# An expert layer whose network turns are woven between the choosing of rows, and 48 gathers ahead of the first store

## The chip, the cores and the metric

One core of one Trainium2 chip runs the whole program. The metric is the device time of one execution in microseconds (us). The engines are PE (TensorE), DVE (VectorE), ACT (ScalarE), POOL (GpSimd) and SP (SyncE, which only issues transfers here). Each engine works through its own instructions in order and meets the others through semaphores.

## The reference

`x` has 32 rows of 120000 samples. They are cut into 938 frames of 128, each frame is turned by an orthonormal cosine basis, and a linear recurrence over the frames of the normalised result is added. The part that matters here is the third step, on `h` of 32 x 938 = 30016 rows of 128:

```python
x_flat = x.reshape(N, Dd)                      # x is the layernorm of h
logits = x_flat @ Wr                           # 8 experts
probs = jax.nn.softmax(logits, axis=0)         # over all rows
vals, idx = jax.lax.top_k(probs.T, C)          # 1024 rows for each expert
selected = x_flat[idx]
h = jax.nn.gelu(jnp.einsum('ecd,edf->ecf', selected, W1) + b1[:, None, :], approximate=False)
out_e = jnp.einsum('ecf,efd->ecd', h, W2) + b2[:, None, :]
weighted = vals[..., None] * out_e
output = jnp.zeros_like(x_flat).at[idx.reshape(-1)].add(weighted.reshape(-1, Dd))
```

Every expert picks its own 1024 rows, so a row can be picked by several experts and the last step is a sum.

## The kernel before

Up to about 350 us the kernel turns, normalises and filters the rows, stores `h` to `out`, and finds for each expert the score at which exactly 1024 rows are in: 13 rounds of counting (`count_round`, L1507 to L1530; the last eight are phase 1). A copy `kept` of `out` is made in the meantime, from which rows are gathered later. The change lies almost wholly in what follows.

The expert part knows 8 experts in 4 pairs, and an expert's 1024 rows as 8 tiles of 128 in two halves `q` of 4 tiles.

- **Choosing.** `extract(pair)` on DVE marks the rows in (two compares L1573), numbers them by a scan (L1576), waits for the PE sums of `offsets(pair)` and makes each row's rank (L1583 to L1603), then `mark(e)` builds a one-hot table for each of the two experts (L1562). PE's `differences(pair)` (L1093) and ACT's `own_steps(pair)` (L822) turn the ranks to steps, PE's `ranks(e, q)` (L1107, eight matmuls) multiplies them with the one-hot table, and `choose(e)` on DVE (L1614 to L1624) makes of each half four columns of `index`.
- **Gathering.** POOL's `find(n)` (L1829) is an indirect DMA of 128 rows from `kept` to `found`. It waits for its half of `index`.
- **Network.** `moments_of_found(e)` on DVE (L1632 to L1662, with many tiny steps) needs the eight gathers of the expert, `normalise_rows(e)` on ACT (L829) follows, `ffn_turn(n)` on PE (L1118) turns half an expert, `turned(n)` on ACT (L837) copies it, `up(n)` on PE (L1133) makes four blocks of 128x512, `gelus(n)` on ACT (L848) takes them one by one, and `down(n)` on PE (L1146) is 16 products of 128x128 summed over four. `score_of_found(e)` on DVE (L1670 to L1677) and `weights_of` on ACT (L854, L855: an exponential between two loads of function tables) make the softmax weights, and `answer(e, g)` on DVE (L1683 to L1698) adds the bias and multiplies with the weights.
- **Adding.** POOL's `add(e)` issues eight indirect DMAs to `out`: expert 0 stores (L1846), the others accumulate (L1843), and each waits until all earlier ones have landed, because two experts may hold the same row.

The order is written out by hand on every engine. Before the change DVE does pairs 0, 1 and 2 whole, then `softmax_scales`, the moments of expert 0, pair 3, expert 6, and then the networks; half 0 and half 1 of expert 7 are chosen between the answers of experts 1 to 3. PE does the same: all choosing first (with `ranks(7, .)` left out), then for each expert `up, up, down, ffn_turn, down`. ACT has the exponential over all scores (`far`, L861) after `own_steps` of pairs 0 to 2. POOL issues 54 gathers, then `add(0)`, then two gathers after each `add`.

## Time and profile before

| | us |
|---|---|
| time, median of 3 executions | 600.93 |
| lowest and highest | 600.62, 605.86 |
| the profiled execution, first to last instruction (span) | 605.3 |
| of it up to the first gather on POOL | 362.5 |
| from there to the end of the last accumulating DMA's issue | 235.0 |
| from there to the end of the span | 7.8 |
| busy share of the span: PE, DVE, ACT, POOL | 66%, 70%, 48%, 49% |

The profile is one execution. Busy times are of the engine, a gap before an instruction is shown in brackets with what ended it, and "remote" or "another core or an unknown queue" means that the semaphore rose at a moment at which no recorded instruction ended. A time of an instruction is from the start of the span.

### The profile page before, as it was taken

How to read it: one execution, taken by the hardware profiler on the slowest of the kernel's cores; microseconds unless marked ns; L12 is line 12 of the kernel's file. 1: busy time of each engine (PE TensorE's matmuls, PEld its weight loads, DVE VectorE, ACT ScalarE, POOL GpSimd, SP SyncE). 2: the span in 40 equal slices, each digit the busy share in tenths (PEclk: the TensorE clock that was granted, in tenths of full speed). 3: DMA queues.
4: the chain of work that ended last, by engine and by line, in shares of the span. 5: the costliest groups of instructions: out<-in, count | busy, mean ns of one | idle time of the engine just before them, and what ended most of it. 6: DMA issues, size and time to landing. Idle time of an engine off the chain costs nothing.

```text
span 605.3 us, 11347 instructions
## 1 busy us (share of the span) xinstructions
PE 397.3 (66%) x3577; PEld 320.0 (53%) x3577; DVE 425.8 (70%) x1653; ACT 292.2 (48%) x560; POOL 298.7 (49%) x213
## 2 busy tenths in 40 slices
PE   5798898999888889997000033210199989997900
PEld 5786788865877788764000022110057667775700
DVE  3877878898488887898888878911787658866100
ACT  2787840076699740177545500120258667686400
POOL 0467830058478730076000007776235687888774
PEclk9999999999899999999555555555579989999965
DMA  8679606699888227699999501121011344443332
GB/s 162 132 183 272 150 15 162 142 253 241 194 148 148 58 48 157 201 275 254 323 318 318 190 0 44 49 52 48 17 28 61 67 74 67 65 75 44 31 30 22
DMA packets 86116, 77.44 MB, mean 128 GB/s; under 512 B 15022, under 2 KB 82930, under 8 KB 85810
## 3 DMA queue, kind: packets, MB, share of 16 engines
q1 hardware_dynamic: 68674, 64.52, 41.6%
q0 software_dynamic: 10368, 8.40, 9.8%
q10 hardware_dynamic: 7024, 3.89, 2.7%
q8 instruction: 27, 0.44, 0.3%
q14 instruction: 23, 0.19, 0.1%
HBM read 52.27 MB, written 39.39 MB: 151 GB/s over the span
## 4 chain that ended last, share of the span: by engine, by line
PE 32%; DVE 21%; issue 14%; DMA 10%; POOL 10%; ACT 6%; another core or an unknown queue 5%; SPq 1%; ACTq 1%; DVEq 0%; POOLq 0%
PE banks L1003 7%; POOL out L1843 7%; PE banks L1030 5%; PE banks L929 5%; PE banks L1133 4%; PE banks L1146 4%; PE banks L1040 3%; DMA xin<-in_x 3%; ACT xn L680 2%; PE banks L915 2%; DMA ring<-toeplitz 2%; DVE xn L1512 2%; DMA const<-constants 1%; DVE xn L1576 1%
## 5 line engine op out<-in xcount | busy, mean ns | idle before, releaser
L1829 POOL DMA_INDIRECT hid<-kept,index x64 | 65.0, 1015 | 115.6 <-DVE index L1624 97.0
L1214 DVE BATCH_NORM_STATS2 stats<-hid 120x6 f32<-120x128 f32 (+1 forms) x512 | 104.9, 278 | 19.8 <-ACT hid L671 19.4
L1843 POOL DMA_INDIRECT out<-hid,index x56 | 88.6, 1582 | 25.9 <-issue 16.3
L929 PE MATMUL banks<-const,xt 128*120 128x128 f32 x512 | 74.0, 290 | 12.0 <-ACT xt L666 11.5
L775 ACT ACTIVATE xt<-banks 128x480 f32<-128x480 f32 x64 | 36.3, 570 | 84.9 <-PE banks L1030 83.7
L929 PEld LDWEIGHTS banks<-const,xt 128*120 128x120 f32 x512 | 63.9, 192 | 20.7 <-ACT xt L666 14.4
L1751 POOL TENSOR_TENSOR small<-small,powers 120x16 f32<-120x16 f32 (+2 forms) x18 | 47.9, 2662 | 47.1 <-DVE small L1232 47.1
L1819 POOL TENSOR_TENSOR small<-small,powers 120x16 f32<-120x16 f32 x15 | 43.2, 2901 | 41.7 <-DVE small L1232 36.3
L1003 PE MATMUL banks<-xn,ring 122*120 122x128 f32 x512 | 58.9, 276 | 6.3 <-DMA xn<-s 3.1
L1146 PEld LDWEIGHTS banks<-w_ring,xn 128*128 128x128 f32 x512 | 60.5, 196 | 3.9 <-issue 3.9
L1003 PEld LDWEIGHTS banks<-xn,ring 122*120 122x120 f32 x512 | 57.6, 189 | 7.4 <-issue 6.9
L1146 PE MATMUL banks<-w_ring,xn 128*128 128x128 f32 x512 | 61.2, 279 | 0.4 <-issue 0.4
L1133 PE MATMUL banks<-xt,w_ring 128*128 128x512 f32 x128 | 61.2, 613 | 0.0
L848 ACT ACTIVATE xn<-banks,b_cols 128x512 f32<-128x512 f32 x64 | 43.6, 687 | 28.4 <-PE banks L1133 25.0
L1415 DVE TENSOR_TENSOR hid<-hid,banks 120x512 f32 (+1 forms) x64 | 42.5, 685 | 11.4 <-PE banks L1003 10.7
L829 ACT ACTIVATE xn<-hid,xn 128x128 f32<-128x128 f32 x64 | 25.5, 481 | 43.1 <-issue 36.0
L671 ACT ACTIVATE hid<-banks 120x512 f32<-120x512 f32 (+1 forms) x64 | 37.9, 592 | 12.1 <-PE banks L929 12.0
L666 ACT ACTIVATE xt<-banks 128x480 f32<-128x480 f32 x64 | 37.4, 588 | 10.0 <-PE banks L915 10.0
L1070 PE MATMUL banks<-counts,setup 128*128 128x3 f16 x13 | 2.4, 187 | 60.4 <-DVE counts L1522 60.4
L915 PE MATMUL banks<-const,xin 120*128 120x120 f32 x256 | 37.8, 277 | 5.6 <-DMA xin<-in_x 5.3
L680 ACT ACTIVATE xn<-hid,small 120x128 f32<-120x128 f32 (+1 forms) x80 | 39.7, 597 | 1.9 <-DVE small L1333 1.8
L1030 PE MATMUL banks<-const,hid 120*128 120x120 f32 x256 | 39.2, 277 | 1.9 <-DVE hid L1415 1.0
(222 smaller groups left out, 705.1 us busy)
## 6 DMA issues: line engine op xcount, KB each, us to landing
kept<-out SPq DMA_DIRECT2D x1, 15008.0 KB, 50.5
xin<-in_x SPq DMA_DIRECT2D x28, 480.0 KB, 6.9
out<-hid SPq DMA_DIRECT2D x14, 960.0 KB, 11.1
w_ring<-in_L_ffn_W SPq DMA_DIRECT2D x16, 256.0 KB
ring<-toeplitz SPq DMA_DIRECT2D x32, 112.5 KB
toeplitz<-ring SPq DMA_DIRECT2D x6, 545.0 KB, 11.3
out<-hid SPq DMA_DIRECT2D x2, 784.0 KB
xin<-in_x SPq DMA_DIRECT2D x4, 384.0 KB
```

The lines of the kernel that those rows point to most:

```text
L680: ins = act.activation(xn[0:L, :, bass.ds(c * HB + b, 1)].rearrange("p k a -> p (k a)"), hid[:, bass.ds(c * HB + b, 1), :].rearrange("p a ...
L848: act.activation(acts[:, g, f], banks[:, 1 + f, :], ACT.Gelu, bias=b1_cols[:, FC * e + f:FC * e + f + 1]).then_inc(gelu_ready, 1)
L915: mm = pe.transpose(spread_rows[:, a, f], xin[:, n // 4, 2 * (n % 4) + a, f * D:(f + 1) * D], cut["identity"][0:L, 0:L].rearrange("p (q j) ...
L929: mm = pe.matmul(banks[0:L, 2 + n % 4, i * D:(i + 1) * D], xt[:, n % 2, i, :], cut["basis_t"], start=True, stop=True)
L1003: mm = pe.matmul(banks[0:L, 2 + n % 4, q * COLS:(q + 1) * COLS], lags[:, slot, (4 * (n % 2) + q) // WOVEN, 0:L, (4 * (n % 2) + q) % WOVEN] ...
L1030: mm = pe.transpose(banks[:, n % 2, j * L:(j + 1) * L], hid[:, c * HB + 4 * j + n, :], cut["identity"][0:L, 0:L])
L1133: pe.matmul(banks[:, 1 + f, :], w1_ring[:, e % 2, f * P:(f + 1) * P], xt_all[:, g], start=True, stop=True).then_inc(up_ready, 1)
L1146: mm = pe.matmul(banks[:, 5 + g, m * D:(m + 1) * D], acts[:, g, f, m * P:(m + 1) * P], w2_ring[:, e % 2, f, :], start=f == 0, stop=f == FC ...
L1214: ins = dve.bn_stats(stats[:, slot, b, :], hid[:, bass.ds(c * HB + b, 1), :].rearrange("p a k -> p (a k)"))
L1751: pool.tensor_tensor(small[:, slot, 4, columns], small[:, slot, 2, columns], powers[0:L, columns], ALU.pow).then_inc(done, 1)
L1829: pool.indirect_dma_start(found[:, n, :], None, kept, bass.IndirectOffsetOnAxis(ap=index[:, n:n + 1], axis=0)).then_inc(found_in[e], 16)
L1843: pool.indirect_dma_start(rows, at_rows, adds[:, n, :], None, compute_op=ALU.add, oob_is_err=True, bounds_check=ROWS * FRAMES - 1).then_in ...
```

## The change

- **The order on DVE.** `extract` is split in `number(pair)` (compares and scan) and `rank_rows(pair)` (the rest). Pairs 0 and 1 are chosen first, then the moments of expert 0, experts 2 and 3, and from there choosing and networks alternate: pair 2 is numbered between the two answers of expert 0, pair 3 after the score of expert 2. From expert 3 on it is answer, answer, score of the next, moments of the one after.
- **The order on PE and ACT.** PE's calls are written out one by one in the same alternation: `offsets(2)` stands behind `up(2)`, `differences(2)` behind `up(3)`, `offsets(3)` behind `up(4)`, `differences(3)` behind `up(5)`. On ACT `own_steps(2)` and `own_steps(3)` stand behind the gelus of experts 1 and 2, `weights_of` is called once for each expert right behind its gelus (before: in five single calls and two double ones with some of them later), and `normalise_rows` of the next expert stands behind it.
- **The order on POOL.** 48 gathers, `add(0)`, the 8 gathers of expert 6, `add(1)`, the 8 gathers of expert 7, then the other adds with nothing between them.
- **The minimum over all scores.** The reduction of 1920 elements on DVE (L1481) is made in eight pieces of 240, one in each round of phase 1; the minimum of the eight pieces follows where the long one stood, which is now behind the first pair's `rank_rows`.
- **Buffers.** The cutoffs are copied from PSUM to SBUF once (`cut_offs`); `normed` has a place of its own; the steps and offsets of pairs 2 and 3 and the ranks of experts 4 to 7 go through bank 7, so `differences(2)` and `(3)` wait until all earlier ranks are used; `up(0)` waits at its fourth block for the copy of the scales (`spread_taken`).

```diff
 BOUND_MARGIN, BOUND_FLOOR = 1.01**2, 1e-12
 NEAREST_OF_BOUND = 0.98 * (1 - 1 / 1.01)
-FOUND_FIRST = 54
-WEIGHED_AFTER = {3: (3, 5), 5: (5, 7), 6: (7, 8)}
-FOUND_BETWEEN = 2
+FOUND_FIRST = 48
+NEAR_PIECES = 8
+NEAR = SEG // NEAR_PIECES
+RANK_COLS = 4 * (L + 2)
 COPIED_ROWS = 512
 RING, SLOTS = 8, 4
 TURN = RING * SLOTS
...
@@ -285,8 +286,7 @@
         acts = xn_all[:, :, :].rearrange("p a b -> p (a b)")[:, 0:2 * FC * 512].rearrange(
             "p (s f n) -> p s f n", s=2, f=FC)
         gone = take("xn", TB * L).rearrange("p (a b) -> p a b", b=L)
-        normed_at = free["xn"][1]
-        work = [take("xn", TB * L) for _ in range(4)]
+        work = [take("xn", TB * L) for _ in range(3)]

         upper, lower = (work[0].bitcast(U16)[:, n * SEG:(n + 1) * SEG] for n in range(2))
         marks = [seen.bitcast(U16)[:, n * SEG:(n + 1) * SEG] for n in range(2)]
@@ -309,6 +309,8 @@
...
+        near = sb("near", [P, NEAR_PIECES])
+        cut_offs = sb("cut_offs", [P, E])
...
@@ -327,13 +328,19 @@
         fstats = take("xn", SLOT_TILES * 6).rearrange("p (m n) -> p m n", m=SLOT_TILES)
         fsmall = take("xn", 3 * 7 * SLOT_TILES).rearrange("p (s n m) -> p s n m", s=3, n=7)
         banks = ctx.enter_context(nc.psum_tensor("banks", [P, 8, 512], F32))
-        def offsets_bank(pair):
-
-            return 0 if pair < PAIRS - 1 else 5
+        def offsets_of(pair):
+
+            if pair < 2:
+                return banks[:, 0, 16 * pair:16 * pair + 10]
+            return banks[:, 7, RANK_COLS + 10 * (pair - 2):RANK_COLS + 10 * (pair - 1)]
+
+        def steps_bank(pair):
+
+            return 1 + pair if pair < 2 else 7

         def rank_bank(e, q):

-            return 6 if q and e < E - 1 else 7
+            return 6 if q and e < 4 else 7

         def logit_bank(c):

...
@@ -854,31 +862,24 @@
                 act.activation(parts[:, first:end, :], scores[:, first:end, :], ACT.Exp).then_inc(weight_ready, end - first)
                 act.activation(sc[:, 7:8], sc[:, 7:8], ACT.Gelu)

-            for pair in range(PAIRS - 1):
-                own_steps(pair)
+            own_steps(0)
             act.wait_ge(far_out, 32)
             act.wait_ge(nearest_ready, 1)
             act.activation(far, far, ACT.Exp, scale=-1.0, bias=sc[:, 10:11], accum_out=sc[:, 4:5]
                            ).then_inc(sum_ready, 1)
             act.activation(sc[:, 7:8], sc[:, 7:8], ACT.Gelu)
+            own_steps(1)
             normalise_rows(0)
             turned(0)
-            own_steps(PAIRS - 1)
             for e in range(E):
                 gelus(2 * e)
-                if e == 1:
-                    weights_of(1, 2)
                 gelus(2 * e + 1)
-                if e == 2:
-                    weights_of(2, 3)
+                if e in (1, 2):
+                    own_steps(e + 1)
+                weights_of(e, e + 1)
                 if e < E - 1:
                     normalise_rows(e + 1)
-                if e == 0:
-                    weights_of(0, 1)
-                if e < E - 1:
                     turned(2 * e + 2)
-                if e in WEIGHED_AFTER:
-                    weights_of(*WEIGHED_AFTER[e])

         @block.tensor
         def _(pe):
@@ -1075,7 +1076,7 @@
             def offsets(pair):

                 pe.wait_ge(totals_ready, pair + 1)
-                into = banks[:, offsets_bank(pair), 16 * pair:16 * pair + 10]
+                into = offsets_of(pair)
                 last = numbered[:, pair, :, :, L - 1:L].rearrange("p k (e h) a -> p h k (e a)", h=2)
                 pe.matmul(into[:, 0:8], half["before"],
                           numbered[:, pair, :, :, L - 1:L].rearrange("p k c a -> p (k c a)"), start=True, stop=False)
...
@@ -1088,8 +1089,10 @@
                 pe.wait_ge(rank_ready, pair + 1)
                 if pair == 0:
                     pe.wait_ge(base_ready, 2)
+                if pair > 1:
+                    pe.wait_ge(row_used, 4 * pair)
                 ranked = rank[:, 4 * pair:4 * pair + 4, :]
-                into = banks[:, 1 + pair, 0:4 * (L + 2)]
+                into = banks[:, steps_bank(pair), 0:RANK_COLS]
                 pe.matmul(into, half["steps"], ranked.rearrange("p a b -> p (a b)"), start=True, stop=False)
                 pe.matmul(into.rearrange("p (e h t) -> p h e t", h=2, t=L + 2)[:, 1], half["wrap"],
                           ranked.rearrange("p (e h) t -> p h e t", h=2)[:, 0], start=False, stop=True
@@ -1100,8 +1103,8 @@
                 if q == 0:
                     pe.wait_ge(onehot_ready, e + 1)
...
-                if e:
-                    pe.wait_ge(row_used, 2 * e + q - (0 if q and e == E - 1 else 1))
+                if e or q:
+                    pe.wait_ge(row_used, 2 * e + q - (1 if e < 4 else 0))
...
                     if n:
                         pe.wait_ge(gelu_ready, FC * (n - 1) + f + 1)
+                    elif f == FC - 1:
+                        pe.wait_ge(spread_taken, 1)
...
                 if n == 1:
-                    pe.wait_ge(row_used, 2 * E - 2)
+                    pe.wait_ge(row_used, 8)
...
-            for pair in range(PAIRS):
-                if pair == 2:
-                    pe.wait_ge(peak_ready, 1)
-                    pe.matmul(banks[:, 4, 0:P], cut["group"], peaks, start=True, stop=True).then_inc(peak_spread, 1)
-                if pair == 3:
-                    pe.wait_ge(sum_ready, 1)
-                    pe.matmul(banks[:, 4, P:P + 1], cut["group"], sc[:, 4:5], start=True, stop=True).then_inc(sum_spread, 1)
-                    pe.wait_ge(spread_in_ready, 2)
-                    pe.matmul(banks[:, 4, 2 * P:2 * P + 2 * E], cut["ones"],
-                              spread_in[:, 1:3, :].rearrange("p a b -> p (a b)"),
-                              start=True, stop=True).then_inc(spread_done, 1)
-                    ffn_turn(0)
-                offsets(pair)
-                differences(pair)
-                for e in (2 * pair, 2 * pair + 1):
-                    if e < E - 1:
-                        for q in range(2):
-                            ranks(e, q)
-            for e in range(E):
...
+            offsets(0)
+            differences(0)
+            ranks(0, 0)
+            peaks_of_group()
+            ranks(0, 1)
+            ranks(1, 0)
+            ranks(1, 1)
+            offsets(1)
+            sum_of_group()
+            differences(1)
+            ranks(2, 0)
+            scales_of_experts()
+            ranks(2, 1)
+            ffn_turn(0)
+            ranks(3, 0)
+            up(0)
+            ranks(3, 1)
+            up(1)
+            down(0)
+            down(1)
+            ffn_turn(2)
+            up(2)
+            offsets(2)
+            up(3)
+            differences(2)
+            ranks(4, 0)
+            down(2)
+            ranks(4, 1)
+            down(3)
+            ranks(5, 0)
+            ranks(5, 1)
+            ffn_turn(4)
+            up(4)
+            offsets(3)
+            up(5)
+            differences(3)
+            ranks(6, 0)
+            down(4)
+            down(5)
+            ranks(6, 1)
+            ffn_turn(6)
+            up(6)
+            ranks(7, 0)
+            up(7)
+            ranks(7, 1)
+            down(6)
+            down(7)
+            for e in range(4, E):
+                ffn_turn(2 * e)
                 up(2 * e)
-                if e == 0:
-                    ranks(E - 1, 0)
                 up(2 * e + 1)
-                if e == 3:
-                    ranks(E - 1, 1)
                 down(2 * e)
-                if e < E - 1:
-                    ffn_turn(2 * e + 2)
                 down(2 * e + 1)

         @block.vector
@@ -1478,7 +1524,7 @@

             def nearest_of_partitions():

-                dve.tensor_reduce(sc[:, 0:1], far, AX.X, ALU.min).then_inc(dve_own, own.one())
+                dve.tensor_reduce(sc[:, 0:1], near[:, :], AX.X, ALU.min).then_inc(dve_own, own.one())
                 dve.wait_ge(dve_own, own.all())
                 dve.tensor_scalar(peaks, cut["identity"], sc[:, 0:1], -1.0, ALU.mult, ALU.mult).then_inc(peak_ready, 1)

@@ -1521,6 +1567,9 @@
                     dve.tensor_scalar(counts[:, 0:1], sc[:, 13:14], 1.0 / PACK, None, ALU.mult)
                     dve.tensor_tensor(counts[:, 1:2], sc[:, 12:13], sc[:, 13:14], ALU.subtract
                                       ).then_inc(count_ready, 1)
+                    if phase:
+                        dve.tensor_reduce(near[:, columns(i, 2, k, 1)], far[:, columns(i, 2 * NEAR, k * NEAR, NEAR)],
+                                          AX.X, ALU.min).then_inc(dve_own, own.one())
                     dve.wait_ge(count_spread, turn - phase)

                     dve.scalar_tensor_tensor(passed[:, :], banks[:, 4, 0:3], wanted_below,
@@ -1532,7 +1581,7 @@
...
-            def extract(pair):
+            def number(pair):

                 cols = slice(4 * pair, 4 * pair + 4)
                 both = lambda a: a.rearrange("p (e h) l -> p e (h l)", h=2)
                 flat = lambda a: a.rearrange("p k c l -> p (k c l)")
-                cutoff = banks[:, 5, 2 * pair:2 * pair + 2].unsqueeze(2).broadcast_to([P, 2, 2 * L])
+                cutoff = cut_offs[:, 2 * pair:2 * pair + 2].unsqueeze(2).broadcast_to([P, 2, 2 * L])
...
+
+            def rank_rows(pair):
+
+                cols = slice(4 * pair, 4 * pair + 4)
                 dve.wait_ge(offsets_ready, pair + 1)
                 by_expert = lambda a: a.rearrange("p (e h) -> p e h", h=2)
                 below_in_front, equal_in_front, below_in_all = (
-                    banks[:, offsets_bank(pair), 16 * pair + a:16 * pair + b] for a, b in ((0, 4), (4, 8), (8, 10)))
+                    offsets_of(pair)[:, a:b] for a, b in ((0, 4), (4, 8), (8, 10)))
                 left = wanted[:, pair, :].unsqueeze(2).broadcast_to([P, 2, 2])
                 dve.tensor_scalar(wanted[:, pair, :], below_in_all, -1.0, float(CAP), ALU.mult, ALU.add
                                   ).then_inc(dve_own, own.one())
@@ -1595,10 +1648,6 @@
...
-                if pair == 3:
-                    pe.wait_ge(sum_ready, 1)
-                    pe.matmul(banks[:, 4, P:P + 1], cut["group"], sc[:, 4:5], start=True, stop=True).then_inc(sum_spread, 1)
-                    pe.wait_ge(spread_in_ready, 2)
...
-            for pair in range(PAIRS - 1):
-                if pair == 2:
-                    nearest_of_partitions()
-                extract(pair)
-                if pair == 2:
-                    nearest_of_experts()
-                choose(2 * pair)
-                choose(2 * pair + 1)
+            def take_scales():
+
+                dve.wait_ge(spread_done, 2)
+                dve.tensor_copy(spread[:, :, :].rearrange("p a b -> p (a b)"),
+                                banks[:, 4, 2 * P:2 * P + 2 * E]).then_inc(spread_taken, 1)
+                dve.wait_ge(spread_taken, 1)
+
+            dve.tensor_copy(cut_offs[:, :], banks[:, 5, 0:E]).then_inc(dve_own, own.one())
+            dve.wait_ge(dve_own, own.all())
+            number(0)
+            rank_rows(0)
+            nearest_of_partitions()
+            choose(0)
+            nearest_of_experts()
+            choose(1)
+            number(1)
+            rank_rows(1)
             softmax_scales()
             moments_of_found(0)
-            extract(PAIRS - 1)
-            choose(E - 2)
+            choose(2)
+            take_scales()
+            choose(3)
+            score_of_found(0)
             moments_of_found(1)
-            score_of_found(0)
-            for e in range(E):
-                if e == 1:
-                    score_of_found(1)
-                    moments_of_found(2)
-                if e == 2:
-                    score_of_found(2)
-                    choose(E - 1, (0,))
-                    moments_of_found(3)
-                if e == 3:
-                    score_of_found(3)
-                    moments_of_found(4)
-                    score_of_found(4)
+            answer(0, 0)
+            number(2)
+            answer(0, 1)
+            rank_rows(2)
+            choose(4)
+            choose(5)
+            score_of_found(1)
+            answer(1, 0)
+            answer(1, 1)
+            moments_of_found(2)
+            score_of_found(2)
+            number(3)
+            rank_rows(3)
+            moments_of_found(3)
+            choose(6, (0,))
+            answer(2, 0)
+            choose(6, (1,))
+            answer(2, 1)
+            choose(7)
+            score_of_found(3)
+            moments_of_found(4)
+            for e in range(3, E):
                 answer(e, 0)
                 answer(e, 1)
-                if e == 3:
-                    choose(E - 1, (1,))
-                if e >= 3 and e + 2 < E:
+                if e + 1 < E:
+                    score_of_found(e + 1)
+                if e + 2 < E:
                     moments_of_found(e + 2)
-                    score_of_found(e + 2)

         @block.gpsimd
         def _(pool):
@@ -1850,13 +1918,11 @@
             pool.wait_ge(kept_in, 16)
             for n in range(FOUND_FIRST):
                 find(n)
-            n = FOUND_FIRST
             for e in range(E):
                 add(e)
-                for _ in range(FOUND_BETWEEN):
-                    if n < E * SLOT_TILES:
-                        find(n)
-                        n += 1
+                first = FOUND_FIRST + e * SLOT_TILES
+                for n in range(first, min(first + SLOT_TILES, E * SLOT_TILES)):
+                    find(n)
             pool.wait_ge(added, 128 * E)
```

## Rows read from the trace of the kernel before

**Rows 1.** The page, part 4: the chain that ended last, shares of the span by engine.

```profile
PE 32%; DVE 21%; issue 14%; DMA 10%; POOL 10%; ACT 6%; another core or an unknown queue 5%; SPq 1%; ACTq 1%; DVEq 0%; POOLq 0%
```

**Rows 2.** POOL's instructions grouped by line: count | busy, mean ns | idle before.

```profile
L1843 POOL DMA_INDIRECT out<-hid,index x56 | 88.6, 1582 | 25.9 <-issue 16.3 <-DMA out<-hid,index 4.9 <-DVE hid L1694 4.7
L1829 POOL DMA_INDIRECT hid<-kept,index x64 | 65.0, 1015 | 115.6 <-DVE index L1624 97.0 <-issue 18.6
```

**Rows 3.** POOL in order of time: start, us, instruction [idle before <- releaser].

```profile
362.53 1.24 POOL L1829 DMA_INDIRECT hid<-kept,index  x1 [79.15 <-DVE index L1624]
...
367.84 2.84 POOL L1829 DMA_INDIRECT hid<-kept,index  x1 [0.30 <-issue]
...
427.98 0.94 POOL L1829 DMA_INDIRECT hid<-kept,index  x1 [6.92 <-DVE index L1624]
...
443.55 0.94 POOL L1829 DMA_INDIRECT hid<-kept,index  x1 [10.89 <-DVE index L1624]
...
459.38 1.02 POOL L1846 DMA_INDIRECT out<-hid,index  x1 [8.65 <-DVE hid L1698]
...
476.17 1.61 POOL L1843 DMA_INDIRECT out<-hid,index  x1 [3.78 <-DVE hid L1694]
...
565.84 1.55 POOL L1843 DMA_INDIRECT out<-hid,index  x1 [2.44 <-DMA out<-hid,index]
...
595.93 1.56 POOL L1843 DMA_INDIRECT out<-hid,index  x1 [0.30 <-issue]
```

**Rows 4.** DVE in order of time: a counting gap, a pair extracted, a half chosen, the minimum.

```profile
349.40 0.22 DVE L1526 SCALAR_TENSOR_TENSOR passed<-banks,sc,const 128x3 f32<-128x3 f32 x1 [0.39 <-PE banks L1070]
...
351.41 1.22 DVE L1573 TENSOR_TENSOR xn<-xn,banks 128x480 f16<-128x480 f32 x2 [0.89 <-PE banks L1073]
352.66 2.16 DVE L1576 TENSOR_TENSOR_SCAN xn<-xin,xn 128x960 f16<-128x960 f16 x1
...
357.17 1.67 DVE L1562 TENSOR_SCALAR ring<-setup,bounds 128x1024 f16<-128x1024 f16 x4
359.87 0.66 DVE L1614 TENSOR_TENSOR xin<-banks,const 128x480 f32<-128x480 f32 x1 [1.03 <-PE banks L1107]
...
361.54 0.65 DVE L1614 TENSOR_TENSOR xin<-banks,const 128x480 f32<-128x480 f32 x1
...
381.67 2.15 DVE L1481 TENSOR_REDUCE sc<-far 128x1 f32<-128x1920 f32 x1
```

**Rows 5.** DVE in order of time: pair 2's halves, the moments of expert 0.

```profile
399.34 0.66 DVE L1614 TENSOR_TENSOR xin<-banks,const 128x480 f32<-128x480 f32 x1 [5.05 <-remote]
...
425.95 0.66 DVE L1614 TENSOR_TENSOR xin<-banks,const 128x480 f32<-128x480 f32 x1 [11.54 <-remote]
...
428.09 1.64 DVE L1632 BATCH_NORM_STATS2 xn<-hid 128x6 f32<-128x128 f32 x8
...
432.96 0.17 DVE L1662 SCALAR_TENSOR_TENSOR xn<-xn 128x8 f32<-128x8 f32 x1
```

**Rows 6.** PE in order of time: the ranks of pair 2, then half networks.

```profile
391.51 2.86 PE L1107 MATMUL banks<-xin,ring 128*128 128x122 f16 x24 [0.71 <-DVE ring L1562]
...
455.57 3.74 PE L1146 MATMUL banks<-w_ring,xn 128*128 128x128 f32 x32
459.21 2.81 PE L1133 MATMUL banks<-xt,w_ring 128*128 128x512 f32 x6
```

**Rows 7.** ACT and DVE groups by line, window 440 to 578 us: count | busy, mean ns | idle before.

```profile
L829 ACT ACTIVATE xn<-hid,xn 128x128 f32<-128x128 f32 x56 | 22.3, 481 | 7.1 <-DVE xn L1662 7.0
L854 ACT ACT_TABLE_LOAD x6 | 7.7, 1283 | 0.1
L1670 DVE SCALAR_TENSOR_TENSOR hid<-hid,xn,wr_all 128x128 f32<-128x128 f32 x64 | 24.5, 445 | 0.0
```

**Rows 8.** Windows: stretch, us, busy of PE, PEld, DVE, ACT, POOL (count), PEclk, DMA, GB/s.

```profile
392.00:426.00 34.00, 3.60 (x31) 3.03 (x29) 5.18 (x19) 4.76 (x5) 22.05 (x24) 0.50 0.18 46
446.00:470.00 24.00, 24.00 (x141) 16.97 (x140) 18.38 (x96) 20.46 (x36) 12.07 (x12) 1.00 0.19 56
```

22 lines of the change are left out of this document (15 added, 7 removed).

## The prediction

> **What bounds the kernel now.** I read the chain that ended last first [rows 1]: PE, DVE and POOL share it, and 5% of it, some 28 us, belongs to no instruction. The chain taken for the last 120 us is POOL's queue alone, so the second view is POOL in order of time [rows 3]. From the first gather (362.53) to the end of the last issue (595.93 + 1.56 = 597.49) are 235.0 us. Its work, with the 0.30 between two issues: 64 gathers at 0.94 + 0.30 = 1.25 are 80.0; 8 stores at 1.02 + 0.30 are 10.6; 56 accumulating ones at 1.55 + 0.30 = 1.86 are 104.2. That is 194.8. Its waits beyond the 0.30: for `index` 6.6 and 10.6, for answers 8.4 and 3.5, together 29.1; for earlier adds to land twice 2.1, so 4.3. The rest, 6.8, are stretched issues, such as the gather of 2.84 at 367.84. So the end of the kernel is POOL's work plus what POOL starves for, and only the starving can be changed.
>
> **Where the starving comes from.** All of it goes back to DVE in pair 2 [rows 5]: three halves begin after waits of 5.05, 11.5 and 11.54 us (the middle one has no row), in sum 28, with "remote" as releaser. PE's matmuls for these halves stand in the trace at 391.51 (24 of them in 2.86 us) [rows 6]; their semaphore rose only when DVE went on. I call this the hold. PE had 3.6 us of work in these 34, at a granted clock of 0.50, the lower level [rows 8]. The gathers went on beside it, so POOL lost less than 28 there, but the moments of expert 0 began at 428.09 [rows 5] instead of near 400, and with them `add(0)`.
> The Trainium skill ("SBUF — State Buffer", Who interferes with whom) says that PE and ACT never wait on anyone for SBUF; this trace shows PE's results late by 28 us, and which resource held them it does not show.
>
> **The change, part by part.**
> *Start.* The copy of the cutoffs adds 0.2 on the path to the first gather. The eight partial minima: 1920 elements took 2.15 at L1481, so 240 take about 0.3, in a gap of 0.39 in which DVE waits for PE's count [rows 4]; hidden at best, 8 x 0.1 = 0.8 if the gap ends late. The long one of 2.15 is gone, the short minimum with its scaling (0.5) stands in the 1.03 before the first half of choosing [rows 4]. I take +0.4: first gather at 362.9.
> *POOL.* The same 64, 8 and 56 issues: 194.8. Gathers of experts 6 and 7 now cover the landing of adds 0 and 1; adds 3 to 7 follow on adds without cover, 5 x 2.2 = 11.0 against 4.3. Stretched issues: 6.8 as before. A bare landing wait is the 2.44 of [rows 3] less 0.30. Busy means of the two kinds of issue: [rows 2]. Bare end: 362.9 + 194.8 + 11.0 + 6.8 = 575.5, and 7.8 to the end of the span: 583.3. To this comes what POOL starves for.
> The long gather of 2.84 began beside pair 1's scan on DVE, and pair 3's scan ran while POOL was idle; now every scan runs beside POOL: one more stretch, 0 to 2, inside the 6.8.
> The Trainium skill (same page and section) lets a DVE instruction with two SBUF inputs contend with GpSimd reads; the long gather agrees. By that rule the sum would be 2 us longer at most.
> *Units of the chain.* A pair: compares and scan 3.4, `rank_rows` 2.1 to the ranks and 1.6 for the one-hot tables [rows 4]. PE `differences` 0.8, ACT `own_steps` 0.6, PE `ranks` 0.4 at the upper level and 0.8 at the lower. Half a choosing: 1.67 from start to start [rows 4], its index after 1.75. Moments 5.0 [rows 5]. Score 8 x 0.38 and two small ones, 3.4; `normalise_rows` 3.2, `weights_of` 2 x 1.28 and two short ones, 3.0 [rows 7]. `down` 3.6, `up` with the turn 4 x 0.9 + 0.4 = 4.0, twice that for both at the lower level of the clock [rows 6, 8]. Answer 1.4, for expert 0 1.8.
> *Up to index 4.* Pair 0 ends at 359, experts 0 and 1 are chosen by 367.6, pair 1 is ready at 375. The moments of expert 0 wait for its eighth gather (8 x 1.25 and the stretched one after 362.9, plus 2.4 to land, as in [rows 3]: 377) and end at 382. Expert 2 is chosen by 385.3. The second half of expert 3 now stands behind `up(0)` on PE: rows normalised from 382, turned from 383.8, PE at the lower level, so about 391, chosen by 393. Then score 0 and moments 1: 401.5. Answer 0, the numbering of pair 2 and answer 0's second half: 409. PE in the meantime: turn 2 at 403.7, `up(2)` to 410; only behind it `offsets(2)`, the ranks at 412.5, `up(3)` with its gelus to 415.3, `differences(2)`, `own_steps(2)`, `ranks(4, 0)`, half a choosing: index 4 at about 418.5. POOL has issued 32 gathers by 362.9 + 40.0 + 3.2 = 406.1. **It starves 12 us.** The other three halves of experts 4 and 5 come every 2 to 4 us, POOL needs one every 5: no wait. Stalled behind the late index are all later gathers and `add(0)`, whose answers are long there.
> *Up to index 6.* 16 gathers and `add(0)` take POOL from 418.5 to 449. DVE: experts 4 and 5 chosen by 428.5, score 1 to 432, answer 1 waits for `weights_of(1)` (3.0), moments 2 to 441, score 2, numbering of pair 3 to 448. ACT stood in `weights_of(1)` until score 1 was there, so the rows of expert 2 are normalised only from 441; turn, `up(4)` on a PE that idled since 428 and starts at the lower level: 450.5; `offsets(3)`, ranks 453, `up(5)` 454; on DVE moments 3 stand in front of `choose(6)`: 459; index 6 at 460. **It starves 11 us.** Index 7 (469) is before the end of `add(1)` (485), and the answers are 20 us and more ahead of their adds from here.
> *Sum.* 583.3 + 12 + 11 = 606 in the span of a profiled execution, against 605.3. The layout saves 28 + 1 (the old starving) and pays 23 of new starving, 6.7 of bare landings and 0.4: a draw. If both clocks are at the upper level throughout, 2 x 3 less: 600. The median of 600.93 is 4.3 under the profiled span; I give the new kernel half of that: 604.
>
> **The rivals.**
> *Faster: the indices come in time.* If index 4 is there by 406 and index 6 by 449 minus the 12 gained, the span is 583.3, 3.6% less; with one of them, 594 to 595. For it: DVE and PE are busy under two thirds in the stretch and PE may run each network faster than my 16 us. Against: `offsets(2)` stands behind `up(2)`, which stands behind moments 1, and these behind score 0; the chain is 12 us too long. It decides where index 4 comes before 410: under 598.
> *Slower: the hold falls on the new chain.* It is a property of this program's traffic, not of the order, or the usual executions of before had less of it than the profiled one. Then up to 28 us are added one to one if it falls between 375 and 460, since every PE step there leads to index 4 or 6; after 470 the answers have 20 us of slack and it costs nothing. 604 + 8 to 28: 612 to 632. For it: gathers run beside PE the whole time, as in the hold. Against: pairs 0 and 1 met no hold beside the same gathers.
> *Slower: PE's clock stays at the lower level.* PE now has short bursts with idle time between them from 383 to 470; before it was continuous from 440 and had 1.00 from 446 [rows 8]. At the lower level throughout up to 470 the chain to index 4 has `up(0)`, `down(0)`, `down(1)`, `up(2)` and `up(3)` longer by 18 us and the one to index 6 by 10: 630; half of it: 617.
> *No change by the partial minima alone.* They are 2.15 us in front of pair 2, now off the path; they can't be told apart.
>
> **How the numbers follow.** The draw (598 to 611) 0.45, of which 0.03 lies under 594.9 and 0.08 over 606.9; the faster rival 0.20; the hold 0.22; the low clock 0.13. A measurement of this kernel can tell about 1%, so faster is under 594.9, slower over 606.9. Faster 0.23, same 0.34, slower 0.43. Predicted is the draw's 604. The range takes in half of the fast rival and most of the slow ones: 588 to 626, which leaves out 0.2. The draw's own range is 598 to 611.
>
> **What would show it.** POOL's waits: one before gather 33 and one before gather 49 with `index` as releaser, of 8 to 15 us each, and five of about 2.2 before adds 3 to 7. No wait of POOL for an answer. DVE's wait before the second half of expert 3 of 4 to 7 us with PE L1107 as releaser. "Remote" waits under 5 us in all; if they are over 10 between 375 and 460, the hold rival holds. A granted clock of 0.50 between 410 and 470 speaks for the clock rival. I am wrong if POOL waits for neither index (then 583 to 595), or if the first gather is later than 364.

## The result, and the profile after

| | before | after |
|---|---|---|
| time, median, us | 601.4 | 623.7 |
| lowest and highest | 600.6, 605.9 | 622.3, 624.2 |
| the profiled execution's span | 605.3 | 622.2 |
| first gather on POOL | 362.5 | 361.4 |
| from there to the end of the last add's issue | 235.0 | 252.1 |
| from there to the end of the span | 7.8 | 8.7 |

The ratio is 1.036, with a 95% interval of 1.032 to 1.040. The change makes the kernel slower by 22 us, against the 604 that I named as likeliest. That is outside the draw's own 598 to 611 and inside the 612 to 632 of the rival in which the hold falls on the new chain. (The 600.93 of the first table was the median of three of these four executions of the kernel before.)

All of it is on POOL after the first gather. Its three groups by line (after; count | busy, mean ns | idle before), the answer to [rows 2]:

```profile
L1911 POOL DMA_INDIRECT out<-hid,index x56 | 88.4, 1579 | 28.1 <-issue 15.5 <-DMA out<-hid,index 12.5
L1897 POOL DMA_INDIRECT hid<-kept,index x64 | 63.6, 993 | 139.9 <-DVE index L1673 121.0 <-issue 18.9
L1914 POOL DMA_INDIRECT out<-hid,index x8 | 9.2, 1152 | 2.4 <-issue 2.4
```

The busy time is that of before: 161.2 against 161.9 us. The waits for an index are 121.0 less the 79.5 in front of the first gather, 41.5; before they were 97.0 less 79.15, 17.9. The waits for an answer, 13.3 before, are gone. The waits for landings are 12.5 against 4.9. So +23.6, -13.3 and +7.6, and less than 1 by busy and issue time: 17.1 us, which is 252.1 - 235.0. POOL of after in order of time, the answer to [rows 3]:

```profile
361.37 1.24 POOL L1897 DMA_INDIRECT hid<-kept,index  x1 [79.50 <-DVE index L1673]
...
403.97 0.95 POOL L1897 DMA_INDIRECT hid<-kept,index  x1 [5.78 <-DVE index L1673]
...
429.22 0.95 POOL L1897 DMA_INDIRECT hid<-kept,index  x1 [20.34 <-DVE index L1673]
...
442.76 0.95 POOL L1897 DMA_INDIRECT hid<-kept,index  x1 [3.85 <-DVE index L1673]
...
476.02 1.00 POOL L1897 DMA_INDIRECT hid<-kept,index  x1 [11.56 <-DVE index L1673]
...
529.74 1.55 POOL L1911 DMA_INDIRECT out<-hid,index  x1 [2.40 <-DMA out<-hid,index]
...
598.91 1.55 POOL L1911 DMA_INDIRECT out<-hid,index  x1 [2.50 <-DMA out<-hid,index]
```

Two waits stand where I had put them, before gathers 33 (429.22) and 49 (476.02), and five landings are bare (the first and the last are shown). Two waits are new: before gather 29 (the second half of expert 3) and before gather 41 (expert 5). What is late in front of them stands on DVE, the answer to [rows 5]:

```profile
386.41 0.66 DVE L1663 TENSOR_TENSOR xin<-banks,const 128x480 f32<-128x480 f32 x1 [3.27 <-remote]
...
401.95 0.66 DVE L1663 TENSOR_TENSOR xin<-banks,const 128x480 f32<-128x480 f32 x1 [13.78 <-remote]
...
440.73 0.66 DVE L1663 TENSOR_TENSOR xin<-banks,const 128x480 f32<-128x480 f32 x1 [7.72 <-remote]
```

That is 24.8 us of "remote" waits up to 460; before had 28. A fourth of 7.86 ends at 519.35, where no add waits for it. And ACT, which takes the blocks of `up(0)`, sees the same:

```profile
389.87 0.69 ACT L856 ACTIVATE xn<-banks,b_cols 128x512 f32<-128x512 f32 x1 [6.46 <-PE banks L1138]
394.10 0.69 ACT L856 ACTIVATE xn<-banks,b_cols 128x512 f32<-128x512 f32 x1 [3.54 <-remote]
398.30 0.69 ACT L856 ACTIVATE xn<-banks,b_cols 128x512 f32<-128x512 f32 x1 [3.51 <-remote]
401.81 0.60 ACT L845 ACTIVATE xt<-banks 128x512 f32<-128x512 f32 x1 [2.83 <-remote]
402.31 0.68 ACT L856 ACTIVATE xn<-banks,b_cols 128x512 f32<-128x512 f32 x1
```

The blocks reach ACT 4.2 us apart; I had counted 1.8 for one at the lower clock. The windows of this stretch and of the next (after; columns as in [rows 8]):

```profile
383.50:402.00 18.50, 6.79 (x20) 3.20 (x20) 1.66 (x6) 2.25 (x4) 11.34 (x12) 0.68 0.17 46
402.00:430.00 28.00, 25.82 (x137) 17.37 (x138) 21.31 (x82) 18.14 (x30) 4.77 (x5) 0.88 0.10 29
```

In the first 18.5 us every engine but POOL stands nearly still beside 12 gathers, and with the last of those gathers PE is busy again. That is the hold of [rows 5, 8] in another place.

### The profile page after: what moved, and what is told of

Same layout as the page of the kernel before. It is cut to its first block, busy times and chain, and to the rows that moved or that the text cites. A ratio compares the mean times of both kernels' runs of the same rounds, so it can differ in the third digit from the quotient of the medians.

```text
span 622.2 us, 11373 instructions
## 1 busy us (share of the span) xinstructions
PE 398.7 (64%) x3577; PEld 318.2 (51%) x3577; DVE 426.5 (69%) x1662; ACT 298.5 (48%) x568; POOL 298.1 (48%) x213
## 4 chain that ended last, share of the span: by engine, by line
PE 28%; issue 21%; DVE 14%; POOL 13%; DMA 12%; ACT 7%; SPq 2%; another core or an unknown queue 2%; ACTq 1%; DVEq 0%; POOLq 0%
POOL out L1911 10%; PE banks L1004 6%; PE banks L1031 5%; PE banks L930 4%; PE banks L1138 4%; PE banks L1041 3%; DMA out<-hid,index 3%; DMA xin<-in_x 3%; DMA ring<-toeplitz 2%; ACT xn L688 2%; PE banks L916 2%; DVE xn L1558 2%; POOL hid L1897 2%; DMA const<-constants 1%
## 5 line engine op out<-in xcount | busy, mean ns | idle before, releaser
L1897 POOL DMA_INDIRECT hid<-kept,index x64 | 63.6, 993 | 139.9 <-DVE index L1673 121.0
L1138 PE MATMUL banks<-xt,w_ring 128*128 128x512 f32 x128 | 68.9, 678 | 18.4 <-ACT xt L845 12.1
L1151 PEld LDWEIGHTS banks<-w_ring,xn 128*128 128x128 f32 x512 | 58.3, 192 | 2.7 <-issue 2.7
L1151 PE MATMUL banks<-w_ring,xn 128*128 128x128 f32 x512 | 58.8, 275 | 0.0
L1138 PEld LDWEIGHTS banks<-xt,w_ring 128*128 128x128 f32 x128 | 25.6, 216 | 47.9 <-issue 33.3
```

The source lines that it names most:

```text
L1138: pe.matmul(banks[:, 1 + f, :], w1_ring[:, e % 2, f * P:(f + 1) * P], xt_all[:, g], start=True, stop=True).then_inc(up_ready, 1)
L1151: mm = pe.matmul(banks[:, 5 + g, m * D:(m + 1) * D], acts[:, g, f, m * P:(m + 1) * P], w2_ring[:, e % 2, f, :], start=f == 0, stop=f == FC ...
L1897: pool.indirect_dma_start(found[:, n, :], None, kept, bass.IndirectOffsetOnAxis(ap=index[:, n:n + 1], axis=0)).then_inc(found_in[e], 16)
```

## The experiments

The runs were made on four chips, here A to D, and the kernel before ran beside them on each. One reading has to stand in front. **The kernel before takes 578.6 us on chip A and 578.0 on D, but 605.9 on B and 605.2 on C** (7, 11, 13 and 1 executions; 576 to 582 on the first two, 602 to 609 on B). The first pair of measurements (601.4 and 623.7) is like B and C. A comparison is therefore only made within one chip. Each chip was used in one sitting only, so the runs do not tell the chip itself from what else went on there at that time; "chip" stands for both.

### Chip A: four variants

**e1: the gathers only after the choosing of experts 0 to 5.**

```diff
             pool.wait_ge(kept_in, 16)
+            pool.wait_ge(index_ready, 12)
```

> The kernel before, but POOL waits until the rows of pairs 0 to 2 are all chosen (index_ready 12) before its first gather, so no gather runs while PE makes the ranks of pair 2. Theory G, the hold on PE needs gathers in flight: DVE's three waits of 28 us in pair 2 shrink to under 1, the twelfth index is there at about 398, 54 gathers follow until about 468, and since POOL's remaining work after them was 142 us, the span is about 611 and the time 613. Theory P, the hold belongs to this place of the program and not to the gathers: the waits stay near 28, the gathers start at about 428 and the time is about 642.

Measured: 610.0 us, one execution, the first gather at 395.15, no "remote" wait of PE's readers. That agrees with theory G, that the hold needs gathers beside PE. But none of the other three runs on this chip has such a wait either, so the run decides nothing by itself; e9 repeats it.

**e2: 28 of the gathers as plain transfers** of consecutive rows, so that the experts' rows are other ones for gathers 17 to 44.

```diff
             def find(n):
...
+                if 16 <= n < 44:
+                    pool.dma_start(found[:, n, :], kept[n * P:(n + 1) * P, :]).then_inc(found_in[e], 16)
+                    return
```

> The kernel before, but the gathers 16 to 43 are plain transfers of 128 consecutive rows of the copy, also issued by POOL (so experts 2 to 5 work on other rows than they should; the work is the same). Theory G1, any transfer from POOL's queue into SBUF at this rate holds PE: the 28 us stay, time near 601. Theory G2, it is the indirect form (an index read and 128 single descriptors): the remote waits in pair 2 fall under 5 us, pair 3 and the answers come 20 us or more earlier and the time falls to about 575 to 585.

Measured: 576.6 us, one execution, 2 under the kernel before on this chip, no hold. Sixteen plain transfers took 9.07 us, where sixteen gathers take 20. POOL gave the time back in waits of 9.04 for an index, 8.85 and 3.00 for answers. It says nothing on the hold, since this chip shows none, but something on the kernel before: without a hold its first answer is there at 430.01 and not at 459.38 [rows 3], and its 54 gathers (67.5 us from about 361.5) fill just the time up to there. This is inferred: no trace of the unchanged kernel was taken on chip A.

**e3: POOL's new order in the kernel before.**

```diff
-FOUND_FIRST = 54
+FOUND_FIRST = 48
...
-            n = FOUND_FIRST
...
-                for _ in range(FOUND_BETWEEN):
-                    if n < E * SLOT_TILES:
-                        find(n)
-                        n += 1
+                first = FOUND_FIRST + e * SLOT_TILES
+                for n in range(first, min(first + SLOT_TILES, E * SLOT_TILES)):
+                    find(n)
```

> The kernel before with POOL's new order alone: 48 gathers, add 0, the gathers of expert 6, add 1, those of expert 7, then add 2 to 7. By my prediction's ledger: the six gathers no longer in front of add 0 would let it start earlier, but its answers come at 459.4 only, so POOL just waits there; six gathers of 1.25 move behind it (+7.5), and five bare landing waits of 2.2 replace two and some shorter ones (+6): 614 in all, with experts 6 and 7 gathered earlier than before and so no wait for their answers. If the landing cover and the place of the gathers were worth nothing: 601.

Measured: 601.2 us against 578.6, a ratio of 1.038 (1.032 to 1.043). The loss of 22.6 is more than the 13 I expected, and its terms are on POOL:

```profile
430.56 1.02 POOL L1846 DMA_INDIRECT out<-hid,index  x1 [3.32 <-DVE hid L1698]
...
485.19 0.94 POOL L1829 DMA_INDIRECT hid<-kept,index  x1 [13.79 <-DVE index L1624]
...
508.06 1.55 POOL L1843 DMA_INDIRECT out<-hid,index  x1 [2.54 <-DMA out<-hid,index]
...
576.45 1.55 POOL L1843 DMA_INDIRECT out<-hid,index  x1 [2.49 <-DMA out<-hid,index]
```

Five bare landings instead of two are 7.6, the wait before the stores 3.3, and 13.8 come because all gathers of expert 7 now stand behind `add(1)`, while DVE of the kernel before chooses the second half of expert 7 only between later answers. That is 24.7, 2 more than the loss. The order on POOL is thus no part that could be taken over by itself: the landings cost 7.6, and the rest is lost where the indices are late.

**e4: the changed kernel with a pause.** POOL waits before gather 17 until experts 0 to 3 are chosen.

```diff
             def find(n):
...
                 if m % 4 == 0:
                     pool.wait_ge(index_ready, 2 * e + m // 4 + 1)
+                if n == 2 * SLOT_TILES:
+                    pool.wait_ge(index_ready, 8)
```

> The changed kernel, but POOL makes no gather of experts 2 and up before the rows of expert 3 are all chosen (index_ready 8), which leaves PE's first network without gathers beside it. Theory G: the remote waits before the two halves of expert 3 (3.3 and 13.8 us) go, its last index comes at about 391 instead of 403.7, POOL resumes there and has issued 32 gathers at about 412, index 4 comes 11 us earlier than 429, unless the hold strikes up(1) and down(0) instead; time 612 to 616. Theory O, the order alone made the kernel slower: the pause of 8 us in POOL comes on top or is absorbed by the later wait, and the time stays at 624 or above.

Measured: 609.1 us, one execution, without a hold. Since e2 and e3 have none on this chip either, the pause gets no credit for that. The run is worth more for another thing: it shows the changed kernel's chain undisturbed. POOL:

```profile
364.18 1.23 POOL L1899 DMA_INDIRECT hid<-kept,index  x1 [79.52 <-DVE index L1673]
...
394.58 1.19 POOL L1899 DMA_INDIRECT hid<-kept,index  x1 [8.59 <-DVE index L1673]
...
419.32 0.94 POOL L1899 DMA_INDIRECT hid<-kept,index  x1 [3.03 <-DVE index L1673]
...
461.77 0.99 POOL L1899 DMA_INDIRECT hid<-kept,index  x1 [10.19 <-DVE index L1673]
```

Counted from the first gather, index 4 lets gather 33 go after 55.1 us and index 6 gather 49 after 97.6. The prediction had 418.5 - 362.9 = 55.6 and 460 - 362.9 = 97.1. In after they are 67.9 and 114.7: the hold adds 12.7 and 17. The 12.7 stand in DVE's rows: the two halves of expert 3 wait 3.27 + 13.78 in after and 0.34 + 4.04 in e4.

### Chip B: the changed kernel again, and its order on POOL

**e5: the changed kernel, unchanged.**

> The changed kernel once more, on the chip on which its relatives are timed, since the kernel before took 578.6 us on one chip and 601.4 on another. Theory H (the hold, PE's results 25 to 28 us late beside the gathers, is there in some executions and not in others, and costs both kernels about as much): without a hold the time is that of the paused variant (609.1) less its later start of 2.8, so 606, range 600 to 609; with a hold 624. Against a kernel before without a hold (578.6) that is a ratio of 1.04 to 1.05, and with a hold on both sides 1.036. Rival B (the change is slower only because the hold falls on its new chain): without a hold it is at most 1% over the kernel before, 575 to 585.

Measured: 621.0 us against 605.9, a ratio of 1.027 (1.021 to 1.032). The kernel before has its hold here too (e8), DVE of e5 waits 2.41, 14.40 and 7.64 for unknown releasers, POOL 19.36 before gather 33 and 11.44 before gather 49. All this is as in the first measurement, so the hold is no accident of one execution. Two more "remote" waits, of 7.25 and 1.21, end at 485.94 and 488.90, beside and just behind the gathers of expert 6.

**e6: the changed kernel with POOL's old order.**

```diff
-FOUND_FIRST = 48
+FOUND_FIRST = 54
...
-                first = FOUND_FIRST + e * SLOT_TILES
-                for n in range(first, min(first + SLOT_TILES, E * SLOT_TILES)):
-                    find(n)
+            n = FOUND_FIRST
...
+                for _ in range(2):
+                    if n < E * SLOT_TILES:
+                        find(n)
+                        n += 1
```

> The changed kernel with POOL's old order: 54 gathers, the stores, then two gathers after each add; all else is the changed kernel. Theory N (the networks between the choosing make the index of expert 6 late, about 98 us after the first gather, and 48 is there to answer that): POOL waits about 23 us before gather 49 with the first stores still behind it, and only then two landings are bare: 361.4 + 98 + 7.5 + 140 + 4 + 8 = 618 us of span at most, 609 at least; time 611 to 620 without a hold, 627 with one: slower than the changed kernel by 5 or more. Rival P (POOL's new order alone is the loss, as it lost 22 us when put into the kernel before): undoing it gives back 20, so 586 without a hold and 603 with one.

Measured: 627.6 us (623.4 to 630.5), a ratio of 1.035 (1.029 to 1.041) to the kernel before and 6.6 over e5. Theory N holds with its number. POOL waits 24.41 us before gather 49, with the first stores still to come. So in the changed kernel 48 gathers ahead are better than 54, and giving POOL its old order back saves nothing. That the new order of the networks must cost time does not follow: e7 keeps it and changes POOL alone.

This trace shows one thing more. The hold came back behind gather 49, with two halves of expert 7:

```profile
492.90 0.66 DVE L1663 TENSOR_TENSOR xin<-banks,const 128x480 f32<-128x480 f32 x1 [8.65 <-remote]
...
504.97 0.66 DVE L1663 TENSOR_TENSOR xin<-banks,const 128x480 f32<-128x480 f32 x1 [10.31 <-remote]
```

and the windows of it:

```profile
488.00:494.00 6.00, 5.00 (x24) 2.24 (x23) 1.00 (x3) 1.37 (x3) 4.47 (x6) 1.00 0.16 55
494.00:500.00 6.00, 3.26 (x27) 2.68 (x25) 0.62 (x3) 1.38 (x3) 4.78 (x5) 1.00 0.15 44
```

The granted clock is 1.00 there, the upper level, and falls to 0.54 only in 500 to 506, when the hold is on. In e5 it is 1.00 as well over the two late waits (480 to 489). The lower clock of [rows 8] is not what makes the hold.

**e7: other places for the adds.** 32 gathers, `add(0)`, 16 gathers, `add(1)`, then 4 gathers after each of adds 1 to 4.

```diff
-FOUND_FIRST = 48
+FOUND_FIRST = 32
+FOUND_AFTER = {0: 16, 1: 4, 2: 4, 3: 4, 4: 4}
...
-                first = FOUND_FIRST + e * SLOT_TILES
-                for n in range(first, min(first + SLOT_TILES, E * SLOT_TILES)):
+            n = FOUND_FIRST
...
+                for _ in range(FOUND_AFTER.get(e, 0)):
                     find(n)
+                    n += 1
```

> The changed kernel with another order on POOL only: 32 gathers, add 0, 16 gathers, add 1, then 4 gathers after each of adds 1 to 4. Theory N (POOL starves before gathers 33 and 49, and the adds are bare behind): add 0 (10.6) fills the first wait, add 1 (14.9) the second, and three of the five bare landings of 2.2 are covered. Without a hold the waits left are 4 before add 0 and 5 before gather 49: span 583, time 585, range 580 to 592; with a hold 602. Rival Q (the answers of experts 0 and 1 are later than I read them, or the stores are slowed by the networks beside them): POOL waits before add 0 and add 1 instead, over 10 us each, and the time is within 1% of the changed kernel.

Measured: 602.0 us (599.4 to 606.1, 10 executions), ratio 0.9945 (0.991 to 0.998) to the kernel before, so half a percent, and 19 us under the changed one. POOL:

```profile
414.56 1.14 POOL L1915 DMA_INDIRECT out<-hid,index  x1 [5.86 <-DVE hid L1748]
...
427.33 0.99 POOL L1898 DMA_INDIRECT hid<-kept,index  x1 [1.49 <-DVE index L1674]
...
473.98 1.02 POOL L1898 DMA_INDIRECT hid<-kept,index  x1 [6.58 <-DVE index L1674]
```

The wait of 19.4 before gather 33 has become 5.9 before the stores and 1.5 before the gather, with the stores done in between; the one before gather 49 fell from 11.4 to 6.6, and three landings are covered. The indices are hardly earlier by it (427.33 is 65.9 after the first gather, 66.6 in e5). The changed order had its early answers to give, and 48 gathers in front of the first store let them lie.

**e8: the kernel before, for its trace.**

> The kernel before, unchanged, to have its trace on this chip. If there is no hold here: no wait with an unknown releaser over 2 us between 380 and 480, POOL's waits for an index or an answer under 3 us in all, span 575 to 578. If there is a hold: some 28 us of such waits on DVE and a span of 600 to 605.

Measured: 606.4 us, span 604.6, with the hold in the same places and sizes as in [rows 5]:

```profile
398.79 0.66 DVE L1614 TENSOR_TENSOR xin<-banks,const 128x480 f32<-128x480 f32 x1 [5.10 <-remote]
413.46 0.66 DVE L1614 TENSOR_TENSOR xin<-banks,const 128x480 f32<-128x480 f32 x1 [12.92 <-remote]
425.37 0.66 DVE L1614 TENSOR_TENSOR xin<-banks,const 128x480 f32<-128x480 f32 x1 [10.16 <-remote]
```

### Chip C: what the hold needs

**e9: e1 once more.**

> The kernel before with POOL waiting, ahead of its first gather, for the twelfth half of the index (experts 0 to 5 chosen), once more, on another chip. It took 610.0 on a chip where the kernel before took 578.6. If the kernel before shows the hold on this chip (over 600): theory G (the hold is something that happens to PE beside the gathers) expects no wait with an unknown releaser in the choosing, the first gather at 395 to 398 and 608 to 614 us, for once as much as on the other chip; theory T (it comes at that time of the program, gathers or not) expects 28 us of such waits before the first gather, which comes at 420 or later, and 635 or more. If the kernel before shows no hold here, this repeats 610.

Measured: 636.9 us against 605.2, one execution each. Neither theory comes out whole. On the mechanism G is right: from the first half of pair 0 to the last half of expert 5 the choosing takes 37.51 us here (360.07 to 397.58) and 37.52 in e1 on chip A, with no unknown wait. The first gather is at 400.22 and not at 395.15 because this execution is 5.1 us later already at the first half. But the time is what T said. The hold starts after the gathers have, and goes on through the 54 of them, now beside pair 3 and the moments of expert 0:

```profile
433.94 0.66 DVE L1614 TENSOR_TENSOR xin<-banks,const 128x480 f32<-128x480 f32 x1 [9.53 <-remote]
454.93 0.66 DVE L1614 TENSOR_TENSOR xin<-banks,const 128x480 f32<-128x480 f32 x1 [19.19 <-remote]
...
461.22 0.17 DVE L1646 SCALAR_TENSOR_TENSOR xn<-xn 128x8 f32<-128x8 f32 x1 [2.23 <-remote]
...
464.03 0.17 DVE L1651 TENSOR_SCALAR xn<-xn 128x8 int32<-128x8 int32 x1 [1.93 <-remote]
...
466.82 0.18 DVE L1656 TENSOR_TENSOR xn<-xn 128x8 f32<-128x8 f32 x1 [2.54 <-remote]
...
469.62 0.17 DVE L1660 SCALAR_TENSOR_TENSOR xn<-xn 128x8 f32<-128x8 f32 x1 [1.93 <-remote]
```

The stores then wait 21.1 us for the first answer. The last four lines wait for DVE's own semaphore, with no work of PE in it. So it is not PE's arithmetic that is held. The same steps are 0.20 us apart at 413.92 to 416.77, beside gathers too, before the hold.

**e10: idle PE filled.** Matmuls that nothing uses, ahead of the offsets and ranks of pairs 1 and 2 of the kernel before.

```diff
+            def fill(count):
+
+                for _ in range(count):
+                    pe.matmul(banks[:, 0, 128:512], half["ones"], keep[:, :, :].rearrange("p a b -> p (a b)")[:, 0:384],
+                              start=True, stop=True)
...
+                if pair in (1, 2):
+                    fill(12)
                 offsets(pair)
...
                         for q in range(2):
+                            if pair in (1, 2):
+                                fill(4)
                             ranks(e, q)
```

> The kernel before with work for PE that nothing uses: 12 matmuls of 384 columns ahead of the offsets of pairs 1 and 2, and 4 ahead of each ranks call of these pairs (0.6 us for four at the upper clock, 1.3 at the lower). Nothing is left out. On a chip with the hold: theory I (the hold comes because PE idles beside the gathers, at the lower clock) expects a granted clock of 1.00 in pair 2, unknown waits under 5 us and 582 to 588 us; theory M (each matmul beside the gathers takes some 1.6 us more, whatever the clock; the trace with the old POOL order shows waits of 8.7 and 10.3 at a clock of 1.00) expects the same 25 to 30 us of such waits or more and 603 to 625. On a chip without it: 579 to 585 by both.

Measured: 595.8 us against 605.2, one execution each. Inconclusive. There are still four "remote" waits on DVE up to 434, of 3.37, 9.43, 4.05 and 4.31, 21 in sum, and the granted clock in pair 2 lay between 0.59 and 0.79 in windows of 8 to 14 us, not at 1.00. More matmuls did not make the hold longer, as theory M wanted. Theory I asked for a clock of 1.00 there, and that was not reached, so it is not tested by this run; what speaks against it are the waits of e6 at 1.00.

**e11: the changed kernel a third time.**

> The changed kernel, for the case that this chip is one on which the kernel before takes 578. Theory H (the hold costs both kernels about as much) then expects 600 to 609, a ratio of 1.04 to 1.05, POOL waits for the index of 8 to 12 us before gather 33 and about 10 before gather 49, and five landing waits of 2.5; rival B (the change is slower only through the hold) 575 to 585. With a hold here: 620 to 625.

Measured: 625.0 us against 605.2. This chip has the hold, so the question for which the run was meant, the changed kernel without one, was not answered. The waits are those of after: 18.63 before gather 33, 12.48 before gather 49.

### Chip D: one step of the order undone

**e12: pair 2 chosen right behind pair 1**, on top of e7, with 46 gathers, `add(0)`, 2 gathers, `add(1)`, then four after each of adds 1 to 4. On DVE:

```diff
             choose(3)
-            score_of_found(0)
-            moments_of_found(1)
-            answer(0, 0)
             number(2)
-            answer(0, 1)
             rank_rows(2)
             choose(4)
             choose(5)
+            score_of_found(0)
+            moments_of_found(1)
+            answer(0, 0)
+            answer(0, 1)
             score_of_found(1)
```

On PE `offsets(2)` stands behind `ranks(3, 1)` and `differences(2)` with expert 4 behind `up(1)`; ACT's `own_steps(2)` follows.

> The changed kernel with two things moved. Pair 2 is chosen right behind pair 1 on every engine (numbering, ranks and both experts ahead of the score of expert 0 and the moments of expert 1; on PE its offsets stand behind the second half of expert 3 and not behind the third half network), and POOL issues 46 gathers, add 0, 2 gathers, add 1, then 4 gathers after each of adds 1 to 4. Theory S (the late index of expert 4 comes from where pair 2's offsets stand in the order) expects: without a hold index 4 at 402 to 405, no wait of POOL before gather 33, under 5 before gather 49, 576 to 584 us, within 1% of the kernel before; with a hold 12 to 15 us of wait at gather 33 instead of 19 to 20, some 3 at gather 49, the answers of expert 0 later by 10 to 20, 590 to 598, faster than the kernel before by 1 to 2.5%. Rival D (the order does not matter, since DVE has the same work up to index 4 and 6): the woven variant's time again, 0.99 to 1.00 of the kernel before with a hold.

Measured: 592.7 us (591.7 to 595.0, 6 executions) against 578.0 on this chip, which has no hold: a ratio of 1.026 (1.022 to 1.029), where I expected 576 to 584. POOL:

```profile
359.51 1.23 POOL L1898 DMA_INDIRECT hid<-kept,index  x1 [79.53 <-DVE index L1674]
...
437.25 1.61 POOL L1912 DMA_INDIRECT out<-hid,index  x1 [2.92 <-DVE hid L1744]
...
465.22 1.03 POOL L1898 DMA_INDIRECT hid<-kept,index  x1 [12.20 <-DVE index L1674]
```

The first half of theory S holds: no wait before gather 33, nor for the first stores. The second fails: index 6 comes 105.7 us after the first gather, 8 later than in e4, and POOL waits 12.2 for it instead of less than 5. What pair 2 gained, pair 3 lost, since its numbering stands behind the same scores, moments and answers. With both pairs in front, as the kernel before has them, POOL met no wait in its first 48 gathers on chip A (e3).

## Why the prediction was right or wrong

**Number and mechanism.** 623.7 lies in the stated 588 to 626 only because the range took in most of the slow rivals. The draw, which had the largest chance and gave the 604, did not come; it is 20 us off. The rival of the hold, given 0.22, came, and with it the forecast is right in its second choice and not in its first.

**The first gather**: 362.9 predicted, 361.4 measured (359.3 to 364.2 in the runs of the changed order). The partial minima cost nothing that shows.

**POOL's ledger** held. Bare landings 5 x 2.2 are 12.5 less 5 x 0.3, 11.0; stretched issues 5.9 against 6.8 (pair 1's scan beside a gather of 2.38, pair 3's beside a store of 1.82; pair 2's found POOL idle); tail 8.7 against 7.8. Without starving the sum was 583.3, and it would have been 361.4 + 194.8 + 11.0 + 5.9 + 8.7 = 581.8.

**The two starvings** were in their places, but larger, and two more came before gathers 29 and 41: 23 predicted, 40.3 measured (41.5 less four times 0.3), 17 us too little. The chain by itself was right, within 0.5 us at both indices, as e4 shows, and between them too: the score and moments behind expert 3 end at 402.3 there, 38.1 after the first gather, where I had 38.6. What came on top is the hold, and it did what the rival said: on the new chain nearly every step of PE leads to index 4 or 6. The "remote" waits are 24.8 us where I had set a bound of 5. The step that failed is that the new chain was taken as free of the hold, and it stands in my words against the rival, "Against: pairs 0 and 1 met no hold beside the same gathers". The hold does not go by pairs. DVE's first such wait begins 18 to 32 us after the first gather (18 in e10, 22 in after, 24 in e9, 32 in [rows 5]), and what stands there meets it.

**"The layout saves 28 + 1 (the old starving)"** is the term that made the draw of it, and it is wrong in kind. I took the hold out of the new kernel and left it in the old. No chip in these runs shows both. Where there is a hold both have it: 601.4 and 623.7, 605.9 and 621.0, 605.2 and 625.0. Where there is none the kernel before takes 578 and not 601. The changed kernel itself was not run on such a chip. An estimate from e4, which is the changed kernel with a pause that index 4 outlasts, is 606 to 609, some 5% over 578.6, and my own sum of 606 for a chain without a hold agrees with it. So the change as a whole costs 15 to 22 us with a hold and, by that estimate, nearer 30 without. How much of it is the order of the networks depends on POOL's order beside it: with the adds of e7 the new order of the networks costs nothing with a hold (602.0 against 605.9), and e12, a relative of e7, costs 14.8 without one.

**The low clock** was given 0.13. It was at 0.50 in 439.3 to 463.2 in after, but in e4, where the clock is also 0.50 from 429.6 to 450.1, index 6 came as I had counted. That rival had no part in the loss. Its own sum is slightly off: 604 + 18 + 10 is 632, and the prediction has 630.

**The showing tests.** DVE's wait before the second half of expert 3 is 4.04 behind PE in e4, in the 4 to 7 given; in after it is 13.78 and "remote". POOL waits for no answer, as said. The five landings are as said. The "remote" sum decided for the rival.

**Rule and trace.** DVE and ACT wait for semaphores that PE or DVE would have raised up to 28 us earlier by their recorded work (454.93 in e9 against 427.32). The longest case in the kernel before is the last half of pair 2, whose matmuls are not among the 24 at 391.51, as the prediction reads, but stand by themselves:

```profile
400.13 0.99 PE L1107 MATMUL banks<-xin,ring 128*128 128x122 f16 x8 [5.75 <-issue]
```

DVE goes on with them at 425.95 [rows 5]. The Trainium skill ("SBUF — State Buffer", Who interferes with whom) says that PE and ACT never wait on anyone. It speaks of ports of SBUF, and these runs don't show that a port is the cause; but a reader who takes the sentence as a promise for PE's results beside gathers would be 13 to 17 us off here, by what the hold adds to the two indices.

## What to carry to other kernels

A wait for nothing that the profile names is no property of the layout until it has been seen to go with it. Before a sum credits a new order with its removal, the old kernel should be compared with itself on another chip, and the same disturbance charged to both sides. And where one queue sets the end, look at what is ready to be put into its gaps before the gaps are made smaller: moving two of the eight blocks of adds into the waits, and spreading the last gathers over the landings, gave back 19 us (e7 against e5), where the change had lost 15 on that chip.
